# A graph network on one core: filling products, three-piece bf16 expansions, self loops joined at the end and a third buffer of gathered rows in the attention walks

## The chip, the cores and the metric

The kernel runs on one core of a Trainium2 chip. The metric is the device time of one execution in microseconds. TensorE (PE in the rows, PEld for its weight loads), VectorE (DVE), ScalarE (ACT), GpSimd (POOL) and SyncE (SP, which only issues transfers here) each run their own queue in order and wait for each other through semaphores.

## The reference, cut to what matters

Four layers, each a graph attention and a feed-forward part with experts, on 3125 nodes with 256 features and 50000 edges sorted by their target `dst`. The change touches the attention of layers 0, 1 and 2, and layer 2 has two such attentions in a row, so there are four of them:

```python
h = einsum('nd,dhf->nhf', x, W)                    # 8 heads of 32
logits = leaky_relu(al_s[src] + al_d[dst], 0.2)    # al_s, al_d: per node and head
m = segment_max(logits, dst)
e = exp(logits - m[dst])
z = segment_sum(e, dst)
out = segment_sum(h[src] * (e / (z[dst] + eps)), dst)
```

In the two attentions of layer 2 (`l2a`, `l2b`) each node has a self loop besides: its edge joins the maximum, the sum and the output. Layers 0 and 1 have none.

## The kernel before, in words

`gat_layer` does one attention in three steps. `project` computes h, al_s and al_d for 25 blocks of 128 nodes, stores the rows of h and al_s to memory (`h_rows`, 272 numbers a row) and keeps al_d in `adn`. `gat_edges` walks over the edges. `finish_gat` divides by the sums and adds the bias.

The walk takes the edges in 416 tiles of 128, and 16 tiles make a chunk: 26 chunks to a walk. No tile mixes two blocks of nodes. The softmax needs one pass only: a running maximum goes from chunk to chunk, and what was already summed for the node on the border is rescaled (`rescale`, L753). For a chunk c:

- POOL gathers the rows of h by `src`, one indirect transfer a tile (L653), into one of two buffers `stage`. From chunk 2 on, the four transfers of a group wait until DVE has used the same group of chunk c-2 (`msg_built`).
- DVE makes a 0/1 matrix `hotT` by node and edge (`nodes_hot`, L672), and PE multiplies it with `adn` (`expand`, L856: 16 products with 8 columns, 16 with self loops), which puts al_d of every edge into `ps_ad`.
- DVE adds al_s, applies the leaky ReLU (`logits`), PE transposes, DVE scans for the maxima in three steps (`tile_ends`, `tile_tops`, `edge_maxima`) with a small product of PE after each, PE transposes back (`turn_maxima`, L877), DVE subtracts (L739), ACT takes the exponential (L828).
- DVE multiplies the gathered rows by the weights, four tiles at a time (`weigh`, L745), and PE multiplies each tile with a 0/1 matrix made by ACT (`scatter`, L890: 264 columns, 272 with self loops), which sums by node. DVE adds each result to `acc` (L764) through four PSUM banks, so the product of tile t waits for the addition of tile t-4.

The order of each queue is written out by hand in `chunk`. The chunks overlap: while chunk c is weighed and scattered in four groups, the maxima of chunk c+1 are worked out between the groups, and the expansion of chunk c+2 stands last. Operands are fp32, and each fp32 product shows as two records in the profile. With self loops (`loops`), the node's own logit is carried through every expansion, joins each tile's logits (`own`, `joined`) and is weighed on the last edge of its node.

## Time and profile before

| | |
|---|---|
| time, median of 3 runs | 7869.34 us (7864.52 to 7906.43) |
| span of the profiled execution, first to last instruction | 7089.8 us |
| difference, outside the span | 779.5 us |
| PE / PEld busy | 5426.1 us (77%) / 3965.8 us (56%) |
| DVE, ACT, POOL busy | 57%, 34%, 41% |
| granted TensorE clock, mean of the span | 0.796 of full |
| the four walks together | 2609.2 us |

The profile has no time of its own for the execution beside its span. All durations below are from this one execution. Shares of the whole span average over stages with different limits, so the walks have to be read by themselves. The profile's chain of what ended last holds one instruction only here and says nothing of the walks; the waits and the timeline of a walk do.

### The profile page before, as it was taken

The numbers are of one execution on the slowest core, as the hardware profiler recorded it, in microseconds if no ns is written. First come the engines' busy times: TensorE is split into PE (matmuls) and PEld (weight loads), VectorE is DVE, ScalarE is ACT, GpSimd is POOL, SyncE is SP. The second block draws the span as 40 slices with busy tenths as digits, with TensorE's granted clock in tenths as the row PEclk, the third lists the DMA queues.
The fourth block names the chain that finished last, engine by engine and source line by source line (L and its number), as shares of the span: only waits on it lengthen the run. The fifth ranks groups of instructions, "written<-read, shape, count | busy, mean of one in ns | idle before, by whom it ended". The sixth has DMA issues, their size and how long they took to land. (4 is left out here: it accounts for less than half of the span.)

```text
span 7089.8 us, 85054 instructions
## 1 busy us (share of the span) xinstructions
PE 5426.1 (77%) x21265; PEld 3965.8 (56%) x21266; DVE 4048.3 (57%) x8410; ACT 2394.9 (34%) x5747; POOL 2934.6 (41%) x2894
## 2 busy tenths in 40 slices
PE   0788759458886678875888488888979998476998
PEld 0566436346664555654666344446768887354776
DVE  5466733356664447764777577762147776794112
ACT  0333212123332133332333255542205554362333
POOL 1566432336660056644666277760007776000000
PEclk9666659766667866766766699998989999796999
DMA  3433323233440044433334111110019999461000
GB/s 89 124 115 116 70 79 110 80 93 114 117 103 12 2 123 114 117 93 98 115 115 100 41 30 32 31 19 18 7 48 345 353 357 254 120 196 16 9 13 23
DMA packets 455428, 710.74 MB, mean 100 GB/s; under 512 B 105113, under 2 KB 334039, under 8 KB 455015
## 3 DMA queue, kind: packets, MB, share of 16 engines
q0 software_dynamic: 142432, 380.88, 19.8%
q1 hardware_dynamic: 310442, 318.36, 14.1%
q10 hardware_dynamic: 2304, 8.52, 0.3%
q8 instruction: 114, 1.87, 0.1%
q14 instruction: 136, 1.11, 0.1%
HBM read 604.94 MB, written 102.97 MB: 100 GB/s over the span
## 5 line engine op out<-in xcount | busy, mean ns | idle before, releaser
L653 POOL DMA_INDIRECT l_edges_stage<-l_h_rows,src_t x832 | 831.9, 1000 | 463.5 <-issue 238.9
L890 PE MATMUL l_edges_ps_sum<-l_edges_msg,l_edges_hot 128*128 128x264 f32 x1664 | 741.2, 609 | 172.2 <-DVE l_attn_acc L764 157.1
L2086 POOL DMA_INDIRECT l_edge_kv<-l_kv_rows,src_t x416 | 465.1, 1118 | 741.0 <-POOLq L1999 557.2
L2522 POOL DMA_INDIRECT l_gate_edges_srow<-l_gate_src_rows,l_gate_edges_idx x512 | 567.6, 1109 | 251.4 <-issue 155.8
L890 PEld LDWEIGHTS l_edges_ps_sum<-l_edges_msg,l_edges_hot 128*128 128x128 f32 x1664 | 446.4, 291 | 373.2 <-DVE l_attn_acc L764 276.9
L2656 PE MATMUL l_gate_edges_ps<-l_gate_edges_wide,l_gate_edges_hot_lo 128*128 128x500 f32 x1024 | 487.0, 633 | 127.3 <-DVE l_gate_edges_wide L2584 127.3
L653 POOL DMA_INDIRECT l2a_edges_stage<-l2a_h_rows,src_t x416 | 414.0, 995 | 236.8 <-issue 114.7
L653 POOL DMA_INDIRECT l2b_edges_stage<-l2b_h_rows,src_t x416 | 413.2, 993 | 237.4 <-issue 116.8
L890 PE MATMUL l2b_edges_ps_sum<-l2b_edges_msg,l2b_edges_hot 128*128 128x272 f32 x832 | 355.3, 581 | 87.6 <-DVE l2b_attn_acc L764 79.8
L890 PE MATMUL l2a_edges_ps_sum<-l2a_edges_msg,l2a_edges_hot 128*128 128x272 f32 x832 | 353.9, 579 | 87.6 <-DVE l2a_attn_acc L764 77.7
L2656 PEld LDWEIGHTS l_gate_edges_ps<-l_gate_edges_wide,l_gate_edges_hot_lo 128*128 128x128 f32 x1024 | 204.9, 205 | 369.6 <-issue 214.5
L764 DVE TENSOR_TENSOR l_attn_acc<-l_attn_acc,l_edges_ps_sum 128x264 f32 x832 | 350.4, 421 | 79.4 <-DVE l_attn_acc L764 34.1
L2187 PE MATMUL l_edge_ps_e<-l_edge_w,l_edge_eaT 128*128 128x256 f32 x1664 | 377.0, 380 | 0.0
L2307 DVE SCALAR_TENSOR_TENSOR l3f_acc<-l_experts_psb,l3f_g,l3f_acc 128x256 f32<-128x256 f32 x200 | 96.8, 484 | 444.7 <-PE l_experts_psb L2338 444.6
L2187 PEld LDWEIGHTS l_edge_ps_e<-l_edge_w,l_edge_eaT 128*128 128x128 f32 x1664 | 317.8, 191 | 43.9
L890 PEld LDWEIGHTS l2b_edges_ps_sum<-l2b_edges_msg,l2b_edges_hot 128*128 128x128 f32 x832 | 204.1, 271 | 198.0 <-DVE l2b_attn_acc L764 153.7
L2368 ACT ACTIVATE l_experts_hT<-l_experts_psa,l_experts_sc_pair 128x320 f32<-128x320 f32 x320 | 197.5, 617 | 343.3 <-PE l_experts_psa L2329 323.3
L890 PEld LDWEIGHTS l2a_edges_ps_sum<-l2a_edges_msg,l2a_edges_hot 128*128 128x128 f32 x832 | 201.7, 268 | 198.5 <-DVE l2a_attn_acc L764 155.6
L2584 DVE TENSOR_TENSOR l_gate_edges_wide<-l_gate_edges_hot_hi,l_gate_edges_val 128x500 f32<-128x500 f32 x512 | 307.6, 674 | 6.4
L1133 PE MATMUL l_agg_ps<-l_agg_msg,l_agg_hot 128*128 128x264 f32 x832 | 209.0, 409 | 82.8 <-DVE l_attn_acc L1098 69.2
L856 PE MATMUL l_edges_ps_ad<-l_attn_adn,l_edges_hotT 128*128 x1664 | 250.2, 291 | 28.2 <-DVE l_edges_hotT L672 28.2
L2613 ACT ACTIVATE l_gate_edges_hot_lo<-col,l_gate_edges_nlo 128x128 f32<-128x128 f32 x512 | 156.4, 388 | 338.0 <-PE l_gate_edges_ps L2656 338.0
(745 smaller groups left out, 11376.6 us busy)
## 6 DMA issues: line engine op xcount, KB each, us to landing
l_val_rows<-l_edge_vj SPq DMA_DIRECT2D x104, 512.0 KB, 5.7
l_agg_stage<-l_val_rows SPq DMA_DIRECT2D x52, 1024.0 KB, 5.3
l_edge_ea<-in_edge_attr SPq DMA_DIRECT2D x388, 128.0 KB, 5.1
l_edges_rel_b<-rel_rows SPq DMA_DIRECT2D x52, 512.0 KB, 4.0
l_experts_w<-in_L_ffn_w SPq DMA_DIRECT2D x32, 512.0 KB, 4.6
l_gate_edges_lo_b<-l_gate_edges_lo_rows SPq DMA_DIRECT2D x64, 256.0 KB, 3.2
l_edges_stage<-l_h_rows,src_t POOLq DMA_INDIRECT x832, 2.8
l2a_edges_rel_b<-rel_rows SPq DMA_DIRECT2D x26, 512.0 KB, 4.0
```

Source lines behind the costliest of these rows:

```text
L653: nc.gpsimd.indirect_dma_start(out=stage[:, c % 2, u, :], out_offset=None, in_=h_rows, in_offset=bass.IndirectOffsetOnAxis(ap=K.src_t[:, c ...
L764: nc.vector.tensor_tensor(to, to, ps_sum[u][:], ALU.add).then_inc(added, 1)
L856: last = nc.tensor.matmul(ps_ad[:, u, :], hotT[:, u * P:(u + 1) * P], adn[:, bass.ds(blks[u], 1), :].rearrange("p a h -> p (a h)"), start= ...
L890: nc.tensor.matmul(ps_sum[u][:], hot[:, g, u, :], msg[:, g % 2, u, :], start=True, stop=True).then_inc(summed, 1)
L1133: nc.tensor.matmul(ps[u][:], hot[:, n % 2, u, :], msg[:, n % 2, u, :], start=True, stop=True).then_inc(summed, 1)
L2086: nc.gpsimd.indirect_dma_start(out=kv[:, m, u, :], out_offset=None, in_=kv_rows, in_offset=bass.IndirectOffsetOnAxis(ap=K.src_t[:, n * EB ...
L2187: last = nc.tensor.matmul(ps_e[h][:, u, :], eaT[:, n % ES, 2 * h + u, c, :], w[:, c, :], start=(c == 0), stop=(c == DC - 1))
L2368: nc.scalar.activation(hT[l][:, v % 2, f, half * HALF:(half + 1) * HALF], psa[n % NA][:], ACT.Relu, bias=sc_pair[:, 1, l, v // NG, f:f + 1 ...
L2522: nc.gpsimd.indirect_dma_start(out=srow[:, n % 4, u, :], out_offset=None, in_=src_rows, in_offset=bass.IndirectOffsetOnAxis(ap=idx[:, n * ...
L2584: nc.vector.tensor_tensor(wide[:, s, u], bcast(hot_hi[:, n % 3, u, :], GV), val[:, s, u, :].unsqueeze(1).to_broadcast([P, NT, GV]), ALU.mu ...
L2613: nc.scalar.activation(hot_lo[:, s, u, :], K.col[:], ACT.Abs, bias=nlo[:, n * GB + u:n * GB + u + 1]).then_inc(near_lo, 1)
L2656: nc.tensor.matmul(flat, hot_lo[:, n % 2, u, :], wide[:, n % 2, u].rearrange("p t f -> p (t f)"), start=False, stop=False).then_inc(summed, 1)
```

## The change

- `keep_warm`: PE gets 34 more products a chunk, each of 128x128 ones with 256 columns of ones in bf16, into a PSUM bank that nobody reads: 5 after each of the four groups of `scatter` (at the first three behind the small product of that group) and 14 after `expand`.
- `adp` takes the place of `adn`: al_d is split into three bf16 pieces whose sum is the fp32 number, `hotT` is bf16 too, and a product has 24 columns (3 pieces of 8). DVE adds the pieces with a new reduction (`ad`) in `logits`. In `project`, one copy becomes three copies and two subtractions.
- Self loops leave the walk: `own`, `joined` and their exponentials go, and `last_max` carries the node's maximum to `acc` in their place. `finish_gat` joins the loop with two shares worked out from both maxima.
- `stage` has three buffers, so that a gather waits for chunk c-3. DVE's loop is written out for six chunks instead of two. PE's and ACT's loops keep two.
- `place_f` goes ahead of `turn_maxima`. Small PSUM results are put together in one bank (`ps_w`).

```diff
-        stage = ph.sb("stage", [P, 2, CK, RW])
+        stage = ph.sb("stage", [P, SL, CK, RW])
-        hotT = ph.sb("hotT", [P, CK * P])
+        hotT = ph.sb("hotT", [P, CK * P], BF16)
...
-                        if c >= 2:
-                            pool.wait_ge(msg_built, NG4 * (c - 2) + g + 1)
+                        if c >= SL:
+                            pool.wait_ge(msg_built, NG4 * (c - SL) + g + 1)
...
-                    nc.vector.tensor_tensor(z[:], stage[:, m, :, HW:RW], ps_ad[:, :, 0:HEADS], ALU.add).then_inc(dv, 1)
-                    if loops:
-                        nc.vector.tensor_tensor(own[:, m], ps_ad[:, :, HEADS:AW], bcast(K.lastb_t[:, bass.ds(c * CK, CK)], HEADS), ALU.add).then_inc(dv, 1)
...
+                    nc.vector.tensor_reduce(ad[:], ps_ad[:].rearrange("p k j h -> p k h j"), AX.X, ALU.add).then_inc(dv, 1)
+                    dve.wait_ge(gathered[i % SL], j * (PER // SL * 16 * CK) + (i // SL * 16 * CK + 16 * CK))
...
+                    nc.vector.tensor_tensor(z[:], stage[:, i % SL, :, HW:RW], ad[:], ALU.add).then_inc(dv, 1)
...
+                def keep_warm(n):
+                    for _ in range(n):
+                        nc.tensor.matmul(ps_warm[:], K.warm[:, 0:P], K.warm[:], start=True, stop=True)
...
                     scatter(c, 0)
                     if after >= 1:
                         turn_logits(c + 1, 1 - m)
+                    keep_warm(5)
                     scatter(c, 1)
                     if after >= 1:
                         place_ends(c + 1)
+                    keep_warm(5)
                     scatter(c, 2)
                     if after >= 1:
                         place_tops(c + 1)
+                    keep_warm(5)
                     scatter(c, 3)
                     if after >= 2:
                         blks = block_ids(nc, mybir.EngineType.PE, K, c + 2)
+                    keep_warm(5)
                     if after >= 1:
+                        place_f(c + 1)
                         turn_maxima(c + 1)
-                        place_f(c + 1)
                     if after >= 2:
                         expand(c + 2, m, blks)
+                    keep_warm(14)
```

In `finish_gat` with self loops, the load of the nodes' own rows is needed by the second large product instead of the first:

```diff
-                    dve.wait_ge(own_in, 16)
-                    own = res[:].rearrange("p t (h c) -> p t h c", c=HC)
-                    ch.link(nc.vector.tensor_tensor(own, own, bcast(w, HC), ALU.mult))
-                    ch.link(nc.vector.tensor_tensor(body, body, res[:], ALU.add))
...
+                    ch.note(nc.vector.tensor_tensor(flat.rearrange("p t (h c) -> p t h c", c=C), by_head[:, :, :, 0:C], bcast(share[:, 0], C), ALU.mult))
                     dve.wait_ge(own_in, 16)
+                    mine = own_h[:].rearrange("p t (h c) -> p t h c", c=HC)[:, :, :, 0:C]
+                    ch.note(nc.vector.tensor_tensor(mine, mine, bcast(share[:, 1], C), ALU.mult))
...
+                    ch.link(nc.vector.tensor_tensor(by_row, by_row, mine, ALU.add))
```

On PE, at the end of a chunk in the walk of layer 0, before the change: the last product of the fourth group, the load of the block numbers of chunk c+2 (`blk_row`), the transpose of the maxima (`seg_max`), `place_f` (`f_diag`) and the first of 16 expansions (`hotT`).

```order
L890 MATMUL l_edges_ps_sum<-l_edges_msg,l_edges_hot 128x264
L928 ISA
L928 TENSOR_LOAD blk_row
L877 MATMUL l_edges_ps_y<-ident,l_edges_seg_max 128x128
L881 MATMUL l_edges_ps_x<-l_edges_f_diag,l_edges_first_hot 128x8
L852 REGISTER_ALU
L856 ISA
L856 MATMUL l_edges_ps_ad<-l_attn_adn,l_edges_hotT 128x8
```

The same place after the change (the names are those of the kernel after, and `warm` is the operand of ones):

```order
L900 MATMUL l_edges_ps_sum<-l_edges_msg,l_edges_hot 128x264
L943 ISA
L943 TENSOR_LOAD blk_row
L860 MATMUL l_edges_ps_warm<-warm 128x256 x5
L891 MATMUL l_edges_ps_w<-l_edges_f_diag,l_edges_first_hot 128x8
L887 MATMUL l_edges_ps_w<-ident,l_edges_seg_max 128x128
L863 REGISTER_ALU
L867 ISA
L867 MATMUL l_edges_ps_ad<-l_attn_adp,l_edges_hotT 128x24
```

Five products and `place_f` now stand between the fourth group and the transpose of the maxima, for which DVE waits; and behind the sixteenth expansion stand 14 more, ahead of the first group of the next chunk.

On DVE, between the first and the second weighing of a chunk, before the change:

```order
L753 SCALAR_TENSOR_TENSOR l_attn_acc<-l_edges_ps_x,l_attn_acc 128x264
L675 REGISTER_ALU
L676 ISA
L677 TENSOR_TENSOR l_edges_z<-l_edges_stage,l_edges_ps_ad 128x128
L680 ISA
L681 SCALAR_TENSOR_TENSOR l_edges_lg<-l_edges_z 128x128
L744 REGISTER_ALU
L745 TENSOR_TENSOR l_edges_msg<-l_edges_stage,l_edges_ps_p 128x1056
```

And after it:

```order
L761 SCALAR_TENSOR_TENSOR l_attn_acc<-l_edges_ps_w,l_attn_acc 128x264
L686 REGISTER_ALU
L687 TENSOR_REDUCE l_edges_ad<-l_edges_ps_ad 128x128
L688 ISA
L689 ISA
L690 TENSOR_TENSOR l_edges_z<-l_edges_stage,l_edges_ad 128x128
L691 REGISTER_ALU
L692 SCALAR_TENSOR_TENSOR l_edges_lg<-l_edges_z 128x128
L752 REGISTER_ALU
L753 TENSOR_TENSOR l_edges_msg<-l_edges_stage,l_edges_ps_p 128x1056
```

One reduction more stands ahead of the logits; nothing else in this stretch moved.

## Rows read from the trace of the kernel before

**Rows 1.** Windows of the four walks: us, busy by engine (x instructions), PEclk, DMA, GB/s.

```profile
210.50:859.70 649.20, 537.28 (x1924) 386.61 (x1924) 437.37 (x989) 213.95 (x573) 415.85 (x416) 0.65 0.40 110
1505.00:2153.60 648.60, 536.37 (x1924) 385.80 (x1924) 437.69 (x989) 213.96 (x573) 416.04 (x416) 0.65 0.40 111
2518.50:3174.30 655.80, 540.86 (x1924) 384.01 (x1924) 456.98 (x1067) 232.84 (x677) 413.97 (x416) 0.68 0.40 109
3266.10:3921.70 655.60, 540.53 (x1924) 384.91 (x1924) 457.40 (x1067) 232.33 (x676) 413.23 (x416) 0.68 0.40 109
```

**Rows 2.** Waits in 300:700, some 17 chunks of layer 0: total, times, longest.

```profile
POOL l_edges_stage L653 <- DVE l_edges_msg L745: 52.7, 18, 3.8
PE l_edges_ps_sum L890 <- DVE l_attn_acc L764: 52.3, 52, 1.3
DVE l_edges_local L691 <- PE l_edges_ps_x L863: 36.9, 17, 2.2
DVE l_edges_run L705 <- PE l_edges_ps_y L867: 21.8, 17, 1.3
DVE l_edges_init L722 <- PE l_edges_ps_y L872: 17.6, 17, 1.3
DVE l_edges_x L739 <- PE l_edges_ps_y L877: 11.7, 17, 0.8
DVE l_edges_z L677 <- PE l_edges_ps_ad L856: 6.1, 10, 1.9
```

**Rows 3.** Timeline, one chunk: start us, us, engine, line [idle before].

```profile
500.31 3.25 PE L890 MATMUL l_edges_ps_sum<-l_edges_msg,l_edges_hot 128*128 128x264 f32 x8 [1.32 <-DVE l_attn_acc L764]
...
503.49 1.01 PE L872 MATMUL l_edges_ps_y<-ones,l_edges_spread 8*128 8x1 f32 x4
...
505.29 3.82 PE L890 MATMUL l_edges_ps_sum<-l_edges_msg,l_edges_hot 128*128 128x264 f32 x8 [0.80 <-DVE l_attn_acc L764]
...
507.28 1.28 DVE L672 TENSOR_SCALAR l_edges_hotT<-l_edges_rel_b,row 128x2048 f32<-128x2048 bf16 x1
507.54 1.84 POOL L653 DMA_INDIRECT l_edges_stage<-l_h_rows,src_t  x1 [0.30 <-issue]
...
509.46 4.42 PE L856 MATMUL l_edges_ps_ad<-l_attn_adn,l_edges_hotT 128*128 x32
...
511.80 1.25 DVE L745 TENSOR_TENSOR l_edges_msg<-l_edges_stage,l_edges_ps_p 128x1056 f32<-128x1056 f32 x1
...
513.74 3.87 PE L890 MATMUL l_edges_ps_sum<-l_edges_msg,l_edges_hot 128*128 128x264 f32 x8
...
524.13 0.71 PE L890 MATMUL l_edges_ps_sum<-l_edges_msg,l_edges_hot 128*128 128x264 f32 x2 [1.32 <-DVE l_attn_acc L764]
```

**Rows 4.** Line L928 in 300:700: count, ns min/median/max (PEldq is PE's sequencer).

```profile
L928 PEldq TENSOR_LOAD <-blk_row x17: 1102/1105/1108, 316.2 to 697.5; - x17
```

**Rows 5.** Windows in the same chunk, and in the experts of layer 1.

```profile
502.09:508.91 6.82, 6.03 (x16) 4.03 (x15) 5.10 (x11) 0.54 (x1) 5.41 (x5) 0.50 0.36 102
508.91:512.33 3.42, 3.42 (x30) 3.16 (x28) 2.44 (x6) 2.72 (x9) 1.42 (x2) 1.00 0.69 231
512.33:522.57 10.24, 9.29 (x25) 6.62 (x24) 6.41 (x13) 3.26 (x9) 7.12 (x8) 0.50 0.32 86
2300.00:2400.00 100.00, 100.00 (x417) 79.01 (x417) 13.55 (x28) 25.31 (x48) 0.00 (x0) 1.00 0.00 0
```

**Rows 6.** Groups in 300:700 by line: busy us, mean ns, idle before.

```profile
L653 POOL DMA_INDIRECT l_edges_stage<-l_h_rows,src_t x270 | 270.3, 1001 | 130.2 <-issue 77.5 <-DVE l_edges_msg L745 52.7
```

**Rows 7.** Groups of the whole span by line, costs near the added work.

```profile
L2566 DVE TENSOR_REDUCE l_gate_edges_a_d<-l_gate_edges_picked 128x32 f32<-128x800 f32 x64 | 63.1, 986 | 2.2
```

**Rows 8.** Timeline: the copy of al_d, and the end of the first walk with self loops.

```profile
205.79 0.36 DVE L567 COPY l_attn_adn<-l_proj_h 128x200 f32<-128x200 f32 x1 [26.40 <-ACT l_proj_h L590]
...
3188.60 7.03 DVE L1190 TENSOR_TENSOR l2a_fin_res<-l2a_fin_res,l2a_attn_acc 128x6600 f32<-128x6600 f32 x1 [12.78 <-DMA l2a_fin_res<-l2a_h_rows]
3195.67 7.04 DVE L1191 TENSOR_TENSOR l2a_attn_acc<-l2a_attn_acc,l2a_fin_res 128x6600 f32<-128x6600 f32 x1
...
3203.26 1.40 DVE L1193 RECIPROCAL l2a_fin_r<-l2a_fin_r 128x200 f32<-128x200 f32 x1
3204.70 6.82 DVE L1195 TENSOR_TENSOR l2a_fin_res<-l2a_attn_acc,l2a_fin_r 128x6400 f32<-128x6400 f32 x1
```

**Rows 9.** Timeline 840:862, the last chunk of the first walk.

```profile
844.46 1.25 DVE L745 TENSOR_TENSOR l_edges_msg<-l_edges_stage,l_edges_ps_p 128x1056 f32<-128x1056 f32 x1
...
855.33 2.55 PE L890 MATMUL l_edges_ps_sum<-l_edges_msg,l_edges_hot 128*128 128x264 f32 x8 [0.88 <-DVE l_attn_acc L764]
...
859.24 0.43 DVE L764 TENSOR_TENSOR l_attn_acc<-l_attn_acc,l_edges_ps_sum 128x264 f32 x1 [0.21 <-DVE l_attn_acc L764]
```

More of the change, by code:

```diff
@@ L566, in _ @@
                 dve.wait_ge(h_kept, NT)
[L567 to L571 removed]
+                near = h[:, :, RW:RW + HEADS]
+                left = near
+                for j in range(PIECES):
+                    piece = adp[:, 0:NT, j, :]
+                    ch.link(nc.vector.tensor_copy(piece, left))
+                    if j + 1 < PIECES:
+                        ch.link(nc.vector.tensor_tensor(rest[:], left, piece, ALU.subtract))
+                        left = rest[:]
+                if own is not None:
+                    ch.link(nc.vector.tensor_tensor(own[:], h[:, :, HW:RW], near, ALU.add))
+                    nc.vector.scalar_tensor_tensor(own[:], own[:], 0.2, own[:], ALU.mult, ALU.max)
             @block.tensor
@@ L611, in gat_edges @@
         lg = ph.sb("lg", [P, 2, CK, HEADS])
-        own = ph.sb("own", [P, 2, CK, HEADS]) if loops else None
-        own_x = ph.sb("own_x", [P, 2, CK, HEADS]) if loops else None
-        joined = ph.sb("joined", [P, CK, HEADS]) if loops else None
+        ad = ph.sb("ad", [P, CK, HEADS])
+        last_max = ph.sb("last_max", [P, 2, CK, HEADS]) if loops else None
         local = ph.sb("local", [P, 2, P])
@@ L766, in adds, with chunk @@
                     return add
-                def chunk(c, j, m, after):
-                    jn = j if m == 0 else j + 1
-                    weigh(c, j, m, 0)
+                def chunk(c, j, i, after):
+                    weigh(c, i, 0)
                     blks = block_ids(nc, mybir.EngineType.DVE, K, c)
@@ L1214, in gat_layer @@
     with Phase(nc, name + "_attn") as keep:
-        adn = keep.sb("adn", [P, NT + 1, AW])
+        adp = keep.sb("adp", [P, NT + 1, PIECES, HEADS], BF16)
+        own = keep.sb("own", [P, NT, HEADS]) if loops else None
         with Phase(nc, name + "_nodes") as nodes:
```

183 lines of the change are left out of this document (98 added, 85 removed).

## The prediction, as it was put on record

> **What bounds the kernel now.** I read the windows of the walks first, then the waits of one walk, then the timeline of one chunk, then the granted clock inside it.
>
> The four walks take 649.2, 648.6, 655.8 and 655.6 us, 2609 us or 37% of the span, at a granted clock of 0.65 to 0.68 [rows 1]. Apart from small edits in `project` and `finish_gat` nothing else changes. From one group of products to the same group of the next chunk it is 524.13 - 500.31 = 23.82 us [rows 3]. With self loops the walk is 6.6 us longer over 26 chunks, so I take 24.1 us.
>
> Three queues could set these 23.8 us.
> - POOL: 270 gathers take 270.3 us and 77.5 us of issue, 1.29 us each or 20.6 us for the 16 of a chunk. It waits besides for DVE's weighing, 52.7 us in 17 chunks or 3.1 us each [rows 2, 6]. So POOL follows; its floor is 20.6 us.
> - DVE waits for PE at five places, 36.9 + 21.8 + 17.6 + 11.7 + 6.1 = 94.1 us in 17 chunks, 5.5 us each [rows 2]. Its own work with issue is thus 23.8 - 5.5 = 18.3 us.
> - PE waits for the additions L764 in its turn [rows 2]. A group of four tiles is 8 records and takes some 3.85 us [rows 3], the expansions 4.42 us.
>
> It is a ring through PE and DVE: group of products, small product, scan, first addition, next group. What is slow in it is PE at its lower level. A scatter record takes 3.87/8 = 0.48 us (the last one with its tail; 0.44 us apart), while the experts of layer 1 with 256 or 320 columns run 417 records in 100 us, 0.24 us each, at clock 1.00 [rows 3, 5].
>
> The clock inside a chunk is worth a careful look. It was 0.50 (1.2 GHz) from 502.09 to 508.91, rose to 1.00 (2.4 GHz) at 508.91 right behind the group that had run without a gap from 505.29, and fell again at 512.33. In those 3.42 us PE shows as busy all the time, with 30 records, nearly all of them the 8-column expansions [rows 3, 5]. So busy time does not hold the clock here: wide products raise it, narrow ones behind it let it fall.
>
> **The change part by part.**
>
> Filling products, 34 a chunk. An fp32 product of the experts of some 256 columns shows as two records of 0.24 us at the full level. A bf16 one has never run here. Bounds: half a record and a whole one, so 0.12 to 0.24 us at the full level, 0.22 to 0.48 us at the lower one. I take the lower ends, because a bf16 operand has a single record. That is 4.1 us of PE a chunk at full clock, 7.5 us at half. Most of it lies where PE waits for DVE. What they are to give is the clock: a group of four tiles then takes as long as its additions let it, 2.55 us [rows 9], and not 3.85 us, and the first additions come early enough that DVE's waits for L863, L867 and L872 (36.9 + 21.8 + 17.6 = 76.3 us, 4.5 us a chunk) go, with that for L856.
>
> What becomes late instead. The load of block numbers takes PE's sequencer 1.10 us [rows 4]. Now it lies beside products still running; with short products it lies bare, and behind it stand the 5 fills (0.6 us) and `place_f` before DVE gets the maxima. From the start of L672 that is 1.1 + 0.6 + 0.2 + 0.3 = 2.2 us, and L672 covers 1.28 us of it [rows 3], so the wait at L739 grows from 0.7 to about 0.9 us (1.5 with fills of 0.24 us). If `hotT` in bf16 is made faster (bounds 0.64 to 1.28 us, half and all of the row), that wait grows by the same, and the sum stays.
>
> Three pieces. Expansions go from 32 records to 16: 4.42 us [rows 3] becomes between 2.2 us (the record stays at 0.138) and 4.4 us (the issue of each is the limit); I take 2.2. DVE adds 384 numbers per partition in a reduction: 986 ns for 800 [rows 7] gives 0.47 us, 0.3 to 1.0 us as bounds, on DVE's own path. In `project`, five small operations of 0.36 us [rows 8] replace one, +1.5 us, four times: +6 us. No work hides that.
>
> Self loops. The walk loses two additions of DVE and gets nothing back (`last_max` takes the place of the subtraction L738): worth at most 0.6 us a chunk, about what the reduction costs. In `finish_gat` DVE now stands 12.78 us until the nodes' own rows have come, then runs 7.03, 7.04, 0.5, 1.40 and 6.82 us [rows 8]. After the change the rescaling product (6.8 us), the reciprocal and the small ones run during that load, and behind it come two products of 6.8 us: 13.6 instead of 22.8 us. Gain 9 us, twice: -18 us.
>
> Third buffer. It takes away the 3.1 us for which POOL waits, which nobody waits for now. It matters once the ring is shorter than some 23 us: a gather of two buffers back could only start when its group is weighed. With three, POOL runs at its floor.
>
> DVE's ring at full clock: 18.3 + 0.5 + 0.9 = 19.7 us. PE's part behind the transpose is 16 expansions and 14 fills, 2.2 + 1.7 = 3.9 us, against DVE's subtraction, four additions at 0.43 + 0.21 = 0.64 us and a weighing of 1.25 us [rows 3, 9], 4.1 us. So it is just covered. If the clock falls there, the fills take 3.1 us and PE is 1.2 us late or more. I expect that in most chunks, since the expansions still stand in a row and wide products are thinnest there: 19.7 + 1.5 = 21.2 us for these, and 20.6 us (POOL's floor) for the others. I take 21.0 us.
>
> The sum. Of the 26 chunks the first two are set by the gathers that fill the buffers and stay, so 24 periods count: 24 x (23.8 - 21.0) = 67 us in each of two walks and 24 x (24.1 - 21.0) = 74 us in each of the other two, 283 us. With +6 and -18 it is -295 us on the span of 7089.8. The 779.5 us between the span and the median of the runs I leave as they are: 7869.3 - 295 = 7574, forecast 7575 us. If the outer part were to shrink in proportion, it would be 32 us less.
>
> One rule of the skill speaks for more. The page "TensorE: Matmul & The Clock Gate" of the Trainium skill (section: HAM oscillation — how this bites in real kernels) has the clock fall back when PE idles between bursts. By it a walk filled like this would never fall, and the gathers alone would bound it. The trace disagrees: at 512.33 the clock fell behind a stretch without any idle time [rows 5]. So I give that case less.
>
> Another touches the gathers' floor. A gather that starts beside L672 took 1.84 us and not the usual 0.95 [rows 3]. The page "SBUF — State Buffer" of the Trainium skill (section: Who interferes with whom) says that a VectorE operation in a two-port mode locks GpSimd out while it runs. By it a shorter L672 would lower the floor from 20.6 us towards 16 x 1.25 = 20.0 us, since 0.95 + 0.30 is the gather beside nothing.
>
> **The rivals.**
>
> Gather-bound (chance 0.22). The clock holds, the ring stays at 19.7 us and POOL sets 20.5 us. For it: 1.29 us a gather is steady, and the fills bring wide products to every gap. Against it: expansions in a row let the clock fall. 24 x 3.3 x 2 + 24 x 3.6 x 2 = 331, with the -12 us of the rest 343: 7525 us.
>
> Half a gain (0.15). The clock is full only for part of each chunk, or a fill costs 0.24 us at full level (34 x 0.12 = 4 us more of PE, half of it in waits). Ring 22.7 us: 24 x (1.1 + 1.1 + 1.4 + 1.4) = 120, with 12: 7740 us.
>
> Slower (0.08). The clock stays as it is in rows 1 and the fills lie on the ring. At the lower level five take 1.1 us. Behind the third small product, ended 504.50, PE had 0.79 us until 505.29 [rows 3]: +0.3. Ahead of the transpose nothing hides them: +1.1, with `place_f` +0.4. Behind the expansions: 14 x 0.22 = 3.1 less the 2.2 saved: +0.9. Together +2.8 with the first gap, ring 26.6 us: 24 x (2.8 x 2 + 2.5 x 2) = 254, less 12: 8110 us. It decides itself on the clock: below about 0.7 in the walks the fills cost more than they give. Against it: gapless wide products raised the clock within this chunk, and the fills make more such stretches.
>
> No effect (0.05). The two cancel, or the rings swap: 7830 to 7910 us.
>
> **How the numbers follow.** The forecast has 0.50, with a range of its own of 7530 to 7660 us (ring 20.6 to 22.0). The range for 8 in 10 reaches over the gather-bound case, a floor of 20.0 us and part of the outer share, down to 7490, and up to the half gain at 7745. Beyond 0.5% (39 us), about what a measurement tells from no change: faster 0.50 + 0.22 + 0.14 = 0.86, within 0.06, slower 0.08.
>
> **What would show it.** Right: PEclk of the walks at 0.85 or more, each walk 575 to 590 us, DVE's waits at L697, L712 and L729 nearly gone, POOL's wait for the weighing below 1 us a chunk, the wait of DVE for the transposed maxima the largest left, and the wait for own rows in `finish_gat` under 4 us. Wrong: a clock that stays near 0.66; a POOL that never waits and a DVE that waits for gathers (gather-bound); 14 fills that end after the first weighing in every chunk, with PE's records without a gap (half a gain or slower).

## The result, and the profile after

| | kernel before | kernel after |
|---|---|---|
| time, median of 4 runs each | 7880.51 us (7864.52 to 7906.43) | 8163.35 us (8141.74 to 8193.06) |
| ratio, 95% interval | | 1.036 (1.032 to 1.041) |
| profiled execution: span / own time | 7089.8 us / not known | 8182.8 us / 8184.6 us |

The change made the kernel 3.6% slower; 4% faster was forecast. The last row holds a first hint: the span of the kernel after lies 1.8 us below the time of its own run. In that run nothing like 780 us lies outside the span. What that means for [rows 1] comes out of the experiments.

The windows of the four walks of the kernel after (as [rows 1]: us, busy by engine, PEclk, DMA share, GB/s):

```profile
210.50:1103.80 893.30, 497.08 (x2392) 325.94 (x2392) 434.25 (x1015) 214.62 (x573) 394.22 (x416) 0.73 0.30 81
1760.80:2654.90 894.10, 493.62 (x2392) 325.24 (x2392) 434.28 (x1015) 214.75 (x573) 394.30 (x416) 0.74 0.30 80
3016.30:3895.90 879.60, 505.47 (x2392) 327.01 (x2392) 440.48 (x1041) 232.79 (x677) 396.37 (x416) 0.74 0.31 82
3979.20:4865.00 885.80, 500.67 (x2392) 321.88 (x2392) 441.36 (x1041) 232.04 (x676) 395.71 (x416) 0.75 0.30 81
```

A walk takes 880 to 894 us, a chunk some 33.6 us, though no engine is busy for over 1 us longer than before and the clock is higher (0.73 to 0.75). So an engine waits that did not wait before. Its waits in 300:700, some 12 chunks (total, times, longest):

```profile
POOL l_edges_stage L662 <- DVE l_edges_msg L753: 160.5, 13, 16.5
DVE l_edges_init L729 <- remote: 112.3, 11, 12.4
DVE l_edges_x L747 <- PE l_edges_ps_w L887: 32.5, 12, 3.2
DVE l_edges_run L712 <- remote: 21.3, 9, 2.9
```

"remote" means that no instruction that ended just then explains the release. L729 is the copy of `ps_init` (L722 before), and waits for PE's `place_tops` (L882). The timeline of one chunk, 500:536 (start, us, engine, line, idle before):

```profile
511.39 1.25 DVE L753 TENSOR_TENSOR l_edges_msg<-l_edges_stage,l_edges_ps_p 128x1056 f32<-128x1056 f32 x1
512.91 0.94 POOL L662 DMA_INDIRECT l_edges_stage<-l_h_rows,src_t  x1 [12.85 <-DVE l_edges_msg L753]
514.15 0.94 POOL L662 DMA_INDIRECT l_edges_stage<-l_h_rows,src_t  x1 [0.30 <-issue]
...
521.60 0.27 DVE L712 TENSOR_TENSOR_SCAN l_edges_run<-links_f,l_edges_top,l_edges_ps_w 8x32 f32<-8x32 f32 x1 [2.61 <-remote]
...
526.36 0.60 PE L882 MATMUL l_edges_ps_w<-ones,l_edges_spread 8*128 8x1 f32 x4
...
531.67 0.95 POOL L662 DMA_INDIRECT l_edges_stage<-l_h_rows,src_t  x1 [0.30 <-issue]
535.90 0.16 DVE L729 COPY l_edges_init<-l_edges_ps_w 128x2 f32<-128x2 f32 x1 [10.01 <-remote]
```

PE shows `place_tops` as done at 526.96, yet DVE goes on at 535.90. Once PE's five fills have ended (527.62), only POOL works, whose 16 gathers run without a break from 512.91 to 532.62. In the trace's semaphore events, PE's signals of this stretch (`summed` of the third group and `inits_made`) all come between 535.02 and 535.88. Over the four walks DVE stood for more than 3 us ahead of L729 in 79 of 104 chunks, 773 us in all. All 79 waits ended after the last gather of POOL's run, 3.25 us after the end of its issue and 1.6 us after its landing at the median. That is the pattern; the experiments ask for its cause.

### The profile page after: what moved, and what is told of

Same layout as the page of the kernel before. It is cut to its first block and busy times, and to the rows that moved or that the text cites. A ratio compares the mean times of both kernels' runs of the same rounds, so it can differ in the third digit from the quotient of the medians.

```text
span 8182.8 us, 88730 instructions
## 1 busy us (share of the span) xinstructions
PE 5310.3 (65%) x23137; PEld 3740.9 (46%) x23138; DVE 4023.1 (49%) x8435; ACT 2392.7 (29%) x5749; POOL 2828.9 (35%) x2895
## 3 DMA queue, kind: packets, MB, share of 16 engines
q0 software_dynamic: 142432, 380.88, 17.6%
## 5 line engine op out<-in xcount | busy, mean ns | idle before, releaser
L662 POOL DMA_INDIRECT l_edges_stage<-l_h_rows,src_t x832 | 788.5, 948 | 941.8 <-DVE l_edges_msg L753 623.8
L900 PE MATMUL l_edges_ps_sum<-l_edges_msg,l_edges_hot 128*128 128x264 f32 x1664 | 625.4, 525 | 682.8 <-DVE l_attn_acc L772 442.8
L900 PEld LDWEIGHTS l_edges_ps_sum<-l_edges_msg,l_edges_hot 128*128 128x128 f32 x1664 | 365.7, 245 | 892.5 <-DVE l_attn_acc L772 552.5
L2120 POOL DMA_INDIRECT l_edge_kv<-l_kv_rows,src_t x416 | 444.6, 1069 | 854.1 <-POOLq L2033 562.2
L662 POOL DMA_INDIRECT l2a_edges_stage<-l2a_h_rows,src_t x416 | 396.4, 953 | 452.9 <-DVE l2a_edges_msg L753 294.4
L900 PE MATMUL l2b_edges_ps_sum<-l2b_edges_msg,l2b_edges_hot 128*128 128x272 f32 x832 | 319.6, 533 | 325.3 <-DVE l2b_attn_acc L772 184.1
L900 PE MATMUL l2a_edges_ps_sum<-l2a_edges_msg,l2a_edges_hot 128*128 128x272 f32 x832 | 322.8, 538 | 315.3 <-DVE l2a_attn_acc L772 170.3
L900 PEld LDWEIGHTS l2b_edges_ps_sum<-l2b_edges_msg,l2b_edges_hot 128*128 128x128 f32 x832 | 180.8, 244 | 438.5 <-DVE l2b_attn_acc L772 237.2
L860 PE MATMUL l_edges_ps_warm<-warm 128*128 128x256 bf16 x1768 | 268.6, 297 | 2.3 <-issue 2.3
L753 DVE TENSOR_TENSOR l_edges_msg<-l_edges_stage,l_edges_ps_p 128x1056 f32<-128x1056 f32 x208 | 259.4, 1247 | 18.3 <-issue 18.3
```

Of the source, the lines that this page charges most:

```text
L662: nc.gpsimd.indirect_dma_start(out=stage[:, c % SL, u, :], out_offset=None, in_=h_rows, in_offset=bass.IndirectOffsetOnAxis(ap=K.src_t[:, ...
L753: nc.vector.tensor_tensor(msg[:, g % 2, :, 0:HW].rearrange("p u (h c) -> p u h c", c=HC), stage[:, i % SL, g * GR:(g + 1) * GR, 0:HW].rear ...
L860: nc.tensor.matmul(ps_warm[:], K.warm[:, 0:P], K.warm[:], start=True, stop=True)
L900: nc.tensor.matmul(ps_sum[u][:], hot[:, g, u, :], msg[:, g % 2, u, :], start=True, stop=True).then_inc(summed, 1)
L2120: nc.gpsimd.indirect_dma_start(out=kv[:, m, u, :], out_offset=None, in_=kv_rows, in_offset=bass.IndirectOffsetOnAxis(ap=K.src_t[:, n * EB ...
```

## The experiments

The runs come in five groups, each on a chip of its own with the kernel before timed beside it. On two of the chips the kernel before took 7088 and 7093 us, on the three others 7756, 7872 and 7871 us, like the 7881 us of the table above. I call the first kind of chip undisturbed, the second a chip with the stall. Each chip was used once, so whether the stall belongs to a chip or to the moment (other work on it, for instance) cannot be told apart; "chip" stands for both.

All kernels of the experiments load the block numbers of the sorted experts of layer 0 under a checked bound, which neither the kernel before timed beside them nor the two recorded kernels do. The kernel before with the bound took 26, 14 and 29 us longer than without it (first, third and fourth chip), so the ratios below are some 0.2 to 0.4% too high.

### First chip, undisturbed: 7088.07 us for the kernel before (7076.06 to 7112.75)

**The kernel before again.** No edit but the bound.

> The kernel before, with the block numbers of the sorted experts of layer 0 loaded under a checked bound (some register instructions there, nothing in the walks). The profile of before had a span of 7090 us while its timed runs took 7870; the profile after has 8183 us of span in 8185 us. Theory A (the profiled execution of before was not like its timed runs): this span is near 7860 us, 2 us below the time, and the four walks together take some 780 us more than the 2609 us of that profile, with PE's results held up as in the kernel after. Theory B (780 us lie outside the span of the kernel before): the span is near 7090 again and the walks at 649 and 656 us.

7114.29 us, ratio 1.004 (1.003 to 1.005), span 7112.4 us in its own run, walks of 649 to 653 us. Neither theory fits whole: the span is that of [rows 1 to 9], and nothing but 2 us lies outside it. So the execution of [rows 1 to 9] was one of some 7090 us, and the 780 us are a difference between chips (or moments), not time outside a span.

**The kernel after again.** No edit but the bound.

> The kernel after, with the same checked bound as in the run of the kernel before beside it; a second profile of it on this chip. All theories: 8140 to 8200 us, span 2 us below, the same stalls of DVE before L729. If its span were near 6800 us, stalls would be a matter of the execution and not of the kernel.

6802.58 us (6799.61 to 6806.27), ratio 0.959 (0.957 to 0.962), 285 us less, and 312 us less than the kernel before with the same bound (7114.29 us). The walks and the waits in 300:700:

```profile
208.00:781.30 573.30, 452.51 (x2392) 278.74 (x2392) 434.73 (x1016) 214.55 (x573) 397.89 (x416) 0.92 0.46 125
1446.80:2022.40 575.60, 458.84 (x2392) 282.02 (x2392) 433.81 (x1016) 214.56 (x573) 398.43 (x416) 0.91 0.45 125
2385.70:2971.60 585.90, 446.32 (x2392) 274.70 (x2392) 439.36 (x1042) 233.23 (x677) 402.99 (x416) 0.94 0.45 123
3054.70:3637.00 582.30, 452.35 (x2392) 276.28 (x2392) 439.88 (x1042) 232.07 (x676) 403.69 (x416) 0.93 0.45 123
```

```profile
POOL l_edges_stage L662 <- issue: 95.3, 313, 0.3
DVE l_edges_x L747 <- PE l_edges_ps_w L887: 36.1, 19, 2.0
DVE l_edges_local L697 <- PE l_edges_ps_w L873: 3.8, 7, 1.6
DVE l_edges_init L729 <- PE l_edges_ps_w L882: 3.4, 20, 0.2
POOL l_edges_stage L662 <- DVE l_edges_msg L753: 1.2, 4, 0.3
```

No "remote" is left, and L729 waits 0.2 us. POOL issues gathers without a break here too, so an unbroken run alone does not stall a chip of this kind.

**No fills.** `keep_warm` does nothing:

```diff
-                    for _ in range(n):
-                        nc.tensor.matmul(ps_warm[:], K.warm[:, 0:P], K.warm[:], start=True, stop=True)
+                    pass
```

> The kernel after without the 34 filling products a chunk; all else as after. In the kernel after, the semaphore increments of the third group and of place_tops come 9 us late, some 3.3 us after POOL has issued the last gather of its run. Theory 1 (the fills hold PE up): without them the period falls from 33.5 to below 24 us and the time to 7100 to 7300 us. Theory 2 (gathers in flight hold PE up, fills or not): the period stays at 30 us or more and the time at 7900 to 8150 us. Theory 3 (the fills are harmless and useful, something else is slow): the time rises, clock of the walks back to 0.66.

7067.67 us, ratio 0.997 (0.996 to 0.998), walks of 640 to 656 us at a granted clock of 0.65 to 0.70, as theory 3 had it. Of the 312 us against the kernel before with the same bound 47 are left without the fills.

**Two buffers.**

```diff
-    SL, PER = 3, 6
+    SL, PER = 2, 6
```

> The kernel after with two buffers of gathered rows in place of three (a gather waits for chunk c-2 as before); fills, bf16 pieces and loops as after. Theory 2 says that the run of gathers is what PE stands still for: 16 gathers a chunk are the same, so the time stays within 1% of the kernel after if only their number counts, and falls by 300 us or more if the run ahead of the third buffer is the cause. Theory 1 (fills): no change.

6863.99 us, ratio 0.968 (0.966 to 0.970), walks of 591 to 599 us. The third buffer is worth 61 us on such a chip with the fills; without the fills three buffers, pieces and loops gave 47 us together. There was no stall here for the theories of the expectation to explain.

### Second chip, with the stall: 7755.63 us for the kernel before (7736.76 to 7774.70)

**Turned order.** `place_f` and `turn_maxima` ahead of five of the fills:

```diff
-                    keep_warm(5)
                     if after >= 1:
                         place_f(c + 1)
                         turn_maxima(c + 1)
                     if after >= 2:
                         expand(c + 2, m, blks)
-                    keep_warm(14)
+                    keep_warm(19)
```

> The kernel after, with place_f and turn_maxima of a chunk issued ahead of the five fills that stood before them (the fills are then 19 in one row behind the expansions). In the undisturbed profile of the kernel after DVE waits 1.98 us a chunk before L747 for the turned maxima, and 0.71 us of fills with 0.55 us before them lie in that wait. Theory (the fills in front of turn_maxima lie on the ring): the wait falls to 0.9 to 1.3 us, a chunk takes 20.1 to 20.3 us in place of 20.9, all 104 chunks together save 60 to 80 us: ratio to the kernel before 0.948 to 0.952 on a chip where the kernel after has 0.959. Rival (the ring is set by DVE's own work and the adds, and the wait comes back before the last adds L772): under 15 us, ratio 0.957 to 0.960. If the call meets the chip of the recorded comparison, the kernel before takes 7870 to 7900 and this one 8050 to 8200, with DVE's waits before L729 of 7 to 10 us a chunk as in the recorded profile.

8069.09 us, ratio 1.040 (1.036 to 1.043). The last sentence of the expectation held for this kernel, with chunks of 32.8 to 33.2 us, though the kernel before took 7756 us and not 7870 to 7900. What it was made for, the place of the fills on an undisturbed chip, it could not tell.

**Fills only.** The kernel before with `keep_warm`, its PSUM bank and its calls as after, and nothing else but the shared bank `ps_w` and the order that it asks for.

> The kernel before with the fills alone (and the order place_f, turn_maxima, which the shared bank asks for): float32 expansions, self loops joined in the walk, two buffers. Theory (the fills raise the granted clock and that alone gives most of the gain): mean granted clock of the walks 0.85 or more, a chunk 21.4 to 22.2 us in place of 23.9, time 6870 to 6950, ratio 0.97 to 0.98. Rival (the float32 expansions leave no room for fills, 34 of them cost as much as the clock gives): a chunk 23.5 to 24.5 us, ratio 0.995 to 1.01.

7900.57 us, ratio 1.018 (1.015 to 1.022), chunks of 30.9 to 31.6 us, granted clock of the walks 0.73 to 0.78. This stands for a chip with the stall only; what the fills alone give elsewhere was not run.

**Pieces only.** The two edits of "No fills" and "Two buffers" together.

> The kernel after without the fills and with two chunks of gathered rows: what is left is the expansion in bf16 pieces and the self loops joined at the end. The kernel with three buffers and no fills had 0.9966. Theory (the clock is what the ring waits for): the pieces save DVE and PE work that the low clock gives back; a chunk 23.6 to 24.2 us, ratio 0.995 to 1.005. Rival (shorter expansions and fewer DVE steps show by themselves): a chunk under 23.3 us, ratio under 0.99.

7905.38 us, ratio 1.019 (1.016 to 1.022), chunks of 32.1 to 32.5 us in layers 0 and 1, 30.5 to 30.7 us in layer 2. No fill and no third buffer is needed for the change to lose here.

**Plain rows.** The kernel after:

```diff
-                            nc.gpsimd.indirect_dma_start(out=stage[:, c % SL, u, :], out_offset=None, in_=h_rows,
-                                                         in_offset=bass.IndirectOffsetOnAxis(ap=K.src_t[:, c * CK + u:c * CK + u + 1], axis=0)).then_inc(gathered[c % SL], 16)
+                            row = (c * CK + u) % NT * P
+                            nc.gpsimd.dma_start(stage[:, c % SL, u, :], h_rows[row:row + P, :]).then_inc(gathered[c % SL], 16)
```

> The kernel after with every gather of the walks replaced by a plain transfer of 128 consecutive rows of the same table into the same place, issued on the same queue: the rows gathered are the wrong ones, so what is left out is the choice of rows by index; bytes and order stay. On a chip where the kernel after has 0.959: POOL's 16 gather issues of 0.96 us a chunk vanish; if the gathers cost the ring nothing (the forecast's case), a chunk stays at 20.7 to 21.2 us and the ratio at 0.955 to 0.962; if their landing is part of the ring (the rival bound by gathers), the ratio falls below 0.95. On the chip of the recorded comparison: if the gathers in flight hold PE's signals up, walks of 570 to 600 us in place of 880 and a time under 7100; if the stall comes from elsewhere, walks of 850 us or more.

6809.87 us (6802.78 to 6817.95), ratio 0.878 (0.876 to 0.881): 1259 us less than its neighbour with turned order, on the same chip. Its first walk:

```profile
208.50:764.80 556.30, 451.26 (x2392) 277.67 (x2392) 432.47 (x1016) 214.64 (x573) 221.72 (x416) 0.93 0.42 129
```

Same bytes, same queue, same number of packets on it (142432), same PE and DVE work, and no wait of DVE for "remote". So it is POOL's indirect gathers, not the amount of data moved and not the fills, that stall the walk on such a chip. The plain rows lie one behind the other in memory and take POOL 0.53 us each in place of 0.95; which of the differences counts was not tried.

### Third chip, undisturbed: 7093.10 us for the kernel before (7080.82 to 7100.51)

**The kernel before, for a profile.** No edit but the bound; it serves as the undisturbed partner of the same profile on the fourth chip.

> The kernel before, unchanged, for a profile of it on the chip of this call. Two chips have answered so far: on one it takes 7090 us (chunks of 23.9 us), on the other 7756 us in the call before this and 7880 us in the recorded comparison. If the call meets the second: theory (signals between the engines come late while POOL issues gathers) says that the time lies in the parts that gather and nowhere else: chunks of 29 to 31 us in the walks (+5.5 to +6.5 us, 570 to 650 us over 104 chunks), l_gate and l_edge together 70 to 160 us longer, and every other part (projections, experts, softmax, aggregation) within 5 us of the profile of 7090 us. Rival (the whole chip is slower): every part longer in proportion, 9 to 11%.

7107.21 us, ratio 1.002 (1.001 to 1.003).

**Before with plain rows.** The edit of "Plain rows" on the kernel before.

> The kernel before with every gather of the walks replaced by a plain transfer of 128 consecutive rows (what is left out is the choice of rows by index). The kernel after with the same edit took 6810 us on the chip where the kernel before took 7756. Theory (only the gathers slow the walks there): chunks of 23.4 to 24.2 us and a time of 7060 to 7170 us on either chip, so that between the two kernels without gathers the change is worth -3.5 to -5%, as on the undisturbed chip. Rival (the change gains by what it does to gathers): 6810 to 6950 us, the two kernels alike without them.

7059.61 us, ratio 0.995 (0.993 to 0.996). That is 48 us less than the same kernel with its gathers (7107.21 us): gathers cost the ring little on an undisturbed chip. Against the 6809.87 us of the kernel after with the same edit the change is worth -3.5% once the walks' gathers are out, though the two come from two chips, and `l_gate` and `l_edge` keep their gathers, which on the second chip cost some 45 us.

**Paused.** The kernel after, POOL's loop:

```diff
+                        for n in range(2):
+                            if c + g + n:
+                                pool.wait_ge(paced, 2 * (c * NG4 + g) + n)
+                            nc.gpsimd.memset(idle[:], 0.0).then_inc(paced, 1)
                         for u in range(g * GR, (g + 1) * GR):
```

> The kernel after, where POOL writes an idle tile twice (some 2 us) ahead of each four gathers of the walks: its work a chunk goes from 20 to 28 us, the same gathers in shorter runs. On the chip that takes 7090 us for the kernel before this must be slower than the kernel after: POOL sets the chunk at 28 us, 104 x 7 = 730 us more, about 7530 us. On the other chip, theory (signals are held for as long as an unbroken run of gathers lasts, and pass when POOL pauses): the signals pass in the pauses, a chunk falls from 33 us to 28 to 30 us, 300 to 500 us less than the 8070 to 8160 us of the kernel after. Rival (each gather in flight costs the signals a fixed time, however spaced, or the hold ends only with the last of a chunk's gathers): a chunk of 36 us or more, 8400 us and up.

7515.85 us, ratio 1.059 (1.057 to 1.061), chunks of 28.1 us: on this chip the pause only costs, as worked out.

**Half plain.** Groups 2 and 4 of each chunk plain, 1 and 3 gathered.

> The kernel after with the second and the fourth group of four gathers of each chunk replaced by plain transfers (half of the rows are not those asked for), 8 gathers a chunk in place of 16, in two runs of four. On the chip of 7090 us: no change, chunks of 20.9 us, about 6800 us. On the other chip: theory (the hold grows with the run of gathers, and a run of four ends before the signals that the ring waits for) says chunks of 21 to 24 us, 6800 to 7150 us. Rival (half of the gathers, half of the loss): chunks near 27 us, about 7450 us.

6762.66 us, ratio 0.953 (0.952 to 0.955), chunks of 20.9 to 21.3 us. The walks take 42 us less than with all gathers on the first chip, where no change was expected; why was not tried.

### Fourth chip, with the stall: 7871.69 us for the kernel before (7837.62 to 7917.58)

**The kernel before, for a profile.** No edit but the bound.

> The kernel before, unchanged, for its profile on the chip of this call. On the chip that takes 7090 us for it: nothing new, chunks of 23.9 to 24.1 us. On the chip that takes 7756 to 7880 us: if the gathers are the cause, chunks of 29 to 31 us in the walks, l_gate and l_edge together 70 to 160 us longer, every part without gathers within 5 us of the other chip's profile; if the whole chip is slower, every part longer by 9 to 11%.

7900.68 us, ratio 1.004 (1.000 to 1.007), span 7889.3 us. The walks of layer 0 and `l2a`, then `l_gate` and `l_edge`; first on this chip, then on the third one:

```profile
207.70:1018.60 810.90, 551.79 (x1924) 396.36 (x1924) 434.84 (x987) 214.77 (x573) 399.77 (x416) 0.64 0.32 88
2883.60:3692.10 808.50, 570.40 (x1924) 397.45 (x1924) 455.83 (x1065) 233.42 (x677) 410.65 (x416) 0.63 0.32 89
4666.00:5536.00 870.00, 648.81 (x2160) 362.89 (x2161) 554.35 (x1360) 382.15 (x775) 563.80 (x512) 0.82 0.16 27
6050.00:6830.00 780.00, 670.96 (x3328) 572.50 (x3328) 517.06 (x625) 368.64 (x624) 477.81 (x444) 0.94 0.91 298
```

```profile
209.50:853.00 643.50, 531.79 (x1924) 381.91 (x1924) 436.03 (x987) 214.65 (x573) 416.00 (x416) 0.66 0.41 111
2533.40:3184.90 651.50, 536.41 (x1924) 380.13 (x1924) 456.17 (x1065) 233.42 (x677) 411.51 (x416) 0.69 0.41 110
4005.00:4817.00 812.00, 636.05 (x2160) 357.61 (x2161) 558.17 (x1360) 382.45 (x776) 569.96 (x512) 0.89 0.17 29
5331.00:6049.00 718.00, 654.47 (x3328) 567.59 (x3328) 517.48 (x625) 368.30 (x624) 487.83 (x444) 0.96 0.98 324
```

The spans differ by 7889.3 - 7108.8 = 780.5 us. The four walks have 3248.9 against 2596.5 us, 652 us of it; `l_gate` (512 gathers) has 58 and `l_edge` (416 gathers) 62 us. That leaves 8 us for all the rest, of which the part between the first two walks, with 100 indirect transfers in the experts of layer 0, is 14 us longer and another part 4 us shorter. So only parts with indirect transfers are slower by more than 5 us. And here is how POOL runs in a chunk of the kernel before on this chip:

```profile
505.39 0.94 POOL L653 DMA_INDIRECT l_edges_stage<-l_h_rows,src_t  x1 [11.41 <-DVE l_edges_msg L745]
...
510.64 0.94 POOL L653 DMA_INDIRECT l_edges_stage<-l_h_rows,src_t  x1 [0.56 <-DVE l_edges_msg L745]
...
516.51 0.94 POOL L653 DMA_INDIRECT l_edges_stage<-l_h_rows,src_t  x1 [1.18 <-DVE l_edges_msg L745]
...
523.02 0.16 DVE L722 COPY l_edges_init<-l_edges_ps_y 128x2 f32<-128x2 f32 x1 [0.17 <-PE l_edges_ps_y L872]
523.11 0.95 POOL L653 DMA_INDIRECT l_edges_stage<-l_h_rows,src_t  x1 [1.91 <-DVE l_edges_msg L745]
```

Four runs of four gathers with breaks between them, where the kernel after has one run of sixteen in the chunk above (and in most others). The signal of `place_tops` got through in the break before 523.11: L722 ran at 523.02, having waited 0.17 us.

**Paused, on this chip.** The same kernel as above.

> The kernel after with 2 us of idle work on POOL ahead of each four gathers; on the undisturbed chip it took 7516 us, 28 us a chunk, set by POOL, as worked out. On the chip with the stall: if the signals are held for as long as an unbroken run of gathers lasts, they pass in the pauses and a chunk takes 28 to 30 us, 7600 to 7900 us in all, less than the kernel after there (8070 to 8160); if each gather in flight has its price however spaced, or the hold ends only with the last gather of a chunk, 36 us or more and 8400 us or more.

7656.05 us (7642.49 to 7669.62), ratio 0.971 (0.965 to 0.977), chunks of 28.1 us as on the undisturbed chip. With 8 us more work for POOL a chunk it is 467 us faster than the turned order on this chip, and faster than the kernel before. In 300:700 POOL no longer waits for the weighing, and the copy that stood for 112.3 us (L729 there, L735 here) shows:

```profile
DVE l_edges_init L735 <- PE l_edges_ps_w L888: 2.2, 10, 0.4
DVE l_edges_init L735 <- issue: 0.9, 5, 0.2
```

**Half plain, on this chip.**

> The kernel after with the second and fourth group of four gathers of a chunk replaced by plain transfers (half of the rows are not those asked for); on the undisturbed chip it took 6763 us. On the chip with the stall: 21 to 24 us a chunk and 6900 to 7200 us if a run of four gathers ends before the ring waits for a signal; near 27 us and 7450 us if the loss goes with the number of gathers.

6900.61 us, ratio 0.875 (0.870 to 0.880), chunks of 20.9 to 21.3 us, as undisturbed. With half of the gathers plain, all of the walks' loss is gone, not half of it. A fixed price for each gather is ruled out. Of the 138 us over the same kernel's 6763 us, 121 lie in `l_gate` and `l_edge` and 15 between the first two walks.

**Turned order again.**

> The kernel after with place_f and turn_maxima ahead of the five fills. On the undisturbed chip: 6720 to 6745 us, ratio 0.948 to 0.952, if these fills lie on the ring of the chunk (wait before L747 from 1.9 us to 0.9 to 1.3 us); 6785 to 6800 us, ratio 0.957 to 0.960, if the wait only moves to the adds. On the chip with the stall it took 8069 us against 7756 us for the kernel before, and should again be 1.035 to 1.045 times the kernel before.

8122.82 us, ratio 1.032 (1.026 to 1.037), a little under the 1.035 to 1.045 expected, chunks of 32.6 to 33.2 us. Whether it helps an undisturbed chip stays open: it never ran on one.

### Fifth chip, with the stall: 7870.94 us for the kernel before (7842.84 to 7918.27)

**Pauses of 1 us and of half a us** ahead of each four gathers, in place of 2 us: one `memset` of 1040 or of 480 numbers per partition.

> The kernel after with one idle write of 1 us on POOL ahead of each four gathers of the walks (two writes, 2 us, gave 28.1 us a chunk and 7516 us on an undisturbed chip, 7656 us on one with the stall). POOL's work a chunk is 20.0 + 4.1 = 24.1 us. If 1 us of rest lets the signals pass: 104 x 4.0 = 413 us less than with 2 us, 7100 us on an undisturbed chip, 7240 us on one with the stall (kernel before there 7756 to 7880 us: ratio 0.92 to 0.94). If the hold outlasts 1 us: chunks of 29 us and more there, 7750 us or more.

7523.67 us (7511.32 to 7585.21), ratio 0.955 (0.950 to 0.959), the fastest kernel with all its gathers on a chip with the stall. But chunks took 26.9 to 27.2 us, not 24.1: some signals still come late. In 300:700:

```profile
POOL l_edges_idle L665 <- DVE l_edges_msg L758: 34.4, 10, 5.0
DVE l_edges_local L702 <- remote: 30.3, 6, 6.1
DVE l_edges_init L734 <- remote: 22.9, 7, 5.1
```

> The same with an idle write of 0.45 us: POOL's work a chunk is 20.0 + 2.1 = 22.1 us. If so short a rest lets the signals pass: 7516 - 104 x 6.0 = 6895 us on an undisturbed chip (ratio 0.972, where the kernel after has 0.959), 7035 us on one with the stall (ratio 0.89 to 0.91). If the signals need a longer rest: on the chip with the stall chunks of 29 to 34 us, 7750 to 8200 us, as the kernel after.

8240.70 us, ratio 1.048 (1.043 to 1.053), no better than the kernel after itself (1.036 on its chip), chunks of 34 to 35 us:

```profile
POOL l_edges_idle L665 <- DVE l_edges_msg L758: 141.4, 12, 14.7
DVE l_edges_init L734 <- remote: 122.9, 11, 12.6
```

So behind four gathers a break of 0.5 us was too short, 1 us let most signals pass, and 2 us (on the fourth chip) all that DVE waits for. All versions on chips with the stall, with POOL's waits for the weighing in 300:700 (12 to 14 chunks):

| kernel | POOL's waits | us a chunk |
|---|---|---|
| before | 30 times | 30.5 to 31.0 |
| fills only, two buffers | 29 times | 30.9 to 31.6 |
| pieces only, two buffers | 13 times | 32.1 to 32.5 (layer 2: 30.5 to 30.7) |
| after | 13 times | 33.3 to 33.9 |
| after, pauses of 0.5 us | 12 times, with its short pauses | 33.9 to 34.6 |
| after, pauses of 1 us | 10 times, with its pauses | 26.9 to 27.2 |
| after, pauses of 2 us | none, with its pauses | 28.1 |
| after, half plain | | 20.9 to 21.3 |

The number of waits alone does not put the kernels in order: with fills only POOL waits as often as before, and the kernel lost 1.8%. The length of the runs does better. Counted over the four walks, with a break at each gap over 0.4 us, the gathers go out in 249 runs before (fourth chip), 207 with fills only and 160 with pieces only (second chip), 152 with the turned order (fourth chip) and 137 after, while the walks take 3254, 3312, 3331, 3489 and 3551 us. That is an order found in the traces of several chips and not an experiment, and it holds with the stall alone: in [rows 1 to 9] the kernel before has 149 runs and no late signal.

## Why the prediction was wrong, step by step

**The step that failed** is in the sum: "The 779.5 us between the span and the median of the runs I leave as they are". They were not outside the span. The profile of the fourth chip, whose kernel before takes the same time, shows them as a stall of the walks (652 us), `l_gate` and `l_edge` (120 us), which the execution that was profiled for [rows 1] does not have. The span should have been doubted as a picture of the timed runs: a difference of 11% between a span and its time was in my table, and I had no row for what filled it.

**The second fault followed from it.** "Third buffer. It takes away the 3.1 us for which POOL waits, which nobody waits for now." On an undisturbed chip that is right. On a chip with the stall POOL's breaks are when signals pass, and the change removes them: the kernel after issues its 16 gathers in one run. The sum had no term for a signal that comes late, and that is what the walks stood for: from 3248.9 us (fourth chip) to 3552.8 us (that of the comparison), +304 us, less some 5 us outside them, against 283 us between the two medians. The third buffer is not the only cause, since the pieces with two buffers lose too; there POOL also waits once a chunk only. Which of the shorter steps closes the breaks was not tried one by one, nor was the kernel after with two buffers on such a chip.

**The slower rival** that I wrote down (fills on the ring at the lower clock, 8110 us) came near the number by luck: the clock of the walks rose (0.73 to 0.75, where it had 0.65 to 0.68 stay), and with plain rows on a chip with the stall the same 34 fills stood in walks of 556 to 569 us.

**The rest of the sum, on an undisturbed chip:**
- Clock of the walks: 0.85 or more expected, 0.91 to 0.94 found. A fill takes 0.72/5 = 0.14 us at full level and 1.27/5 = 0.25 us at the lower one; I took 0.12 and 0.22.
- Walks of 575 to 590 us expected, 573 to 586 found. The saving of 283 us was 2596.5 - 2317.1 = 279 us between the third chip and the first; on the first chip alone, from the first gather to the last addition, it was 2603.6 - 2314.3 = 289 us.
- The waits of DVE for `place_ends` and `place_tops` went, and POOL's fell to 1.2 us in 19 chunks; the one for `turn_maxima` is the largest left, as expected, but with 1.9 us a chunk twice the size of my 0.9 us. Part is `hotT`, now 0.75 us in place of 1.28, which covers less. The rest is that the fourth group ends 0.85 us after `hotT` starts:

```profile
515.51 1.28 PE L900 MATMUL l_edges_ps_sum<-l_edges_msg,l_edges_hot 128*128 128x264 f32 x4 [0.22 <-DVE l_attn_acc L772]
515.94 0.75 DVE L682 TENSOR_SCALAR l_edges_hotT<-l_edges_rel_b,row 128x2048 bf16<-128x2048 bf16 x1
517.35 0.71 PE L860 MATMUL l_edges_ps_warm<-warm 128*128 128x256 bf16 x5 [0.55 <-issue]
518.47 1.34 PE L867 MATMUL l_edges_ps_ad<-l_attn_adp,l_edges_hotT 128*128 x16
```

- The expansions take 1.34 us, not 2.2, which made up for it. The reduction takes 0.55 us (0.47 taken).
- The floor of POOL is lower than the 20.6 us of [rows 6]: 16 x (0.957 + 0.30) = 20.1 us, and the gather beside `hotT` takes 1.28 us and not 1.84 as in [rows 3]. With a shorter `hotT` the lock that the page "SBUF — State Buffer" of the Trainium skill (section: Who interferes with whom) describes gets shorter; the trace agrees.
- `project` +1.5 us each as expected. `finish_gat` gave 11 us and not 18: `l2a` 9.2, `l2b` only 2 (below).

In sum 289 + 11 - 6 = 294 us, against 295 forecast and 312 measured between the two kernels with the same bound (7114.29 - 6802.58). Of what is left, 8 us lie in `l_edge`, which the change does not touch. That sum and forecast agree within 1 us is luck in part: the wait for `turn_maxima` and `finish_gat` came out worse than forecast, the expansions and POOL's floor better. The mechanism and its size were right for one kind of chip, and the forecast was for the time on another.

## What to carry to other kernels

A profile whose span lies far below the times shown with it was not taken under the conditions that were timed, so get one that was before you add to its rows or subtract from them. An engine off the critical path may be needed idle: where indirect gathers run beside a chain of small signals, breaks of 1 us after each four of them turned +3.6% into -4.5% on a chip with the stall, while without the stall they should give the whole gain back (an estimate from the pauses of 2 us: 7516 - 104 x 4.0 = 7100 us). Time such a change on more than one chip, since this one was 0.959 on one and 1.036 on another.

## What the runs showed of the hardware that was not expected

- On three of the five chips, and on that of the comparison, signals between engines come late while POOL issues indirect gathers in a row. In the chunk shown, PE had ended the third group by 526.43, but its signals came behind the last landing (534.33), at 535.02 and 535.73 and then 0.04 to 0.06 us apart. A run of 16 (20 us) kept L729 waiting for up to 12.4 us. As many bytes and packets in plain transfers on the same queue held none in the walks. The page "DMA: Bandwidth & Descriptors" of the Trainium skill (section: Why a DMA increments its semaphore by 16 and not by 1) says that all 16 engines post an increment for a transfer issued by GpSimd. By that the plain transfers, which GpSimd issued too, post as many, so the increments alone do not explain the hold. Whether the writing of the descriptors or the reading of scattered rows does, and why on some chips only, no run here shows.
- A long operation of POOL with two inputs stops a short one of DVE. In `finish_gat` of `l2b`, on the undisturbed chip, a 128x200 product that elsewhere takes 0.37 us lasted 12.75 us beside POOL's addition of x and the bias:

```profile
3641.23 13.65 POOL L1198 TENSOR_TENSOR x<-x,l2b_fin_b 128x6400 f32<-128x6400 f32 x1 [55.81 <-DMA l2b_fin_b<-in_L_gnn_b]
3642.35 12.75 DVE L1220 TENSOR_TENSOR l2b_fin_share<-l2b_fin_share,l2b_fin_r 128x200 f32<-128x200 f32 x1
3655.03 0.35 DVE L1221 TENSOR_TENSOR l2b_fin_share<-l2b_fin_share,l2b_fin_r 128x200 f32<-128x200 f32 x1
```

  Before, POOL's addition lay mostly in DVE's wait for the nodes' own rows; with that wait filled it is in the way, and most of the 9 us is lost. By the page "SBUF — State Buffer" of the Trainium skill (section: Who interferes with whom) the one of the two that issues first keeps their shared port for the whole instruction; the two rows agree.
